# Ten hops of a graph kernel joined into one stream of groups, with the next hop's operand split on VectorE inside the stream

## What is computed

```
def step(f, _):                       # layer 0, ten times
    msg = f[src] * edge_weight[:, None]
    agg = segment_sum(msg, dst, num_segments=n)
    f = (1.0 - ALPHA) * agg + ALPHA * feat_0
    return (f, None)
out, _ = scan(step, feat, None, length=10)
...
x = layernorm(x + layer0(x))          # then layer 1 (edge MLP), layer 2, layer 3
agg = segment_sum(features[src] * ci[src][:, None], dst)   # layer 2, once
agg = segment_sum(h[src] * norm[:, None], dst)             # layer 3, once
```

## Time and profile before

| | |
|---|---|
| median of 3 runs | 9384.44 us (9378.69 to 9385.2) |
| profiled execution | 9374.58 us, span 9372.8 us |
| PE busy | 7891.7 us (84% of the span) |
| DVE busy | 6697.0 us (71%) |
| POOL busy | 5318.3 us (57%) |
| ACT busy | 4324.7 us (46%) |
| ten hops, first rounding copy to last add | 1774.1 to 5971.3 us |

### The profile page before, as it was taken

The page is one execution under the profiler, slowest core; times in us unless marked ns, Lnnn a source line. Parts: engine busy times, 40 slices in busy tenths (PEclk is TensorE's granted clock), DMA queues, the critical chain, the costliest instruction groups (busy, mean ns, idle before and its releaser), DMA issues. The chain is left out here.

```text
span 9372.8 us, 552081 instructions
## 1 busy us (share of the span) xinstructions
PE 7891.7 (84%) x229013; PEld 6623.7 (71%) x229013; DVE 6697.0 (71%) x13250; ACT 4324.7 (46%) x9003; POOL 5318.3 (57%) x5427
## 2 busy tenths in 40 slices
PE   4957667798989989898988989599999999598595
PEld 4956657798988889898988889444444444387494
DVE  6788888887877878787877878644444444586487
ACT  1249879644444444444444444244444444343142
POOL 2410000276766767676766767477777777375074
PEclk6569955699999999999999999799999999798597
DMA  5300055698988989898988989633332233196195
GB/s 83 97 22 0 6 182 228 252 312 284 312 287 291 304 282 312 285 313 286 311 285 292 300 284 312 184 77 79 79 79 77 77 80 79 41 306 215 60 317 165
DMA packets 572216, 1835.96 MB, mean 196 GB/s; under 512 B 215006, under 2 KB 276470, under 8 KB 570238
## 3 DMA queue, kind: packets, MB, share of 16 engines
q1 hardware_dynamic: 492926, 1779.79, 57.0%
q0 software_dynamic: 59776, 46.03, 3.4%
q10 hardware_dynamic: 19328, 7.36, 0.5%
HBM read 1667.65 MB, written 160.19 MB: 195 GB/s over the span
## 5 line engine op out<-in xcount | busy, mean ns | idle before, releaser
L1282 POOL TENSOR_TENSOR arena<-arena 128x768 f32<-128x768 f32 (+2 forms) x1800 | 2739.5, 1522 | 2821.8 <-DVE arena L1338 2804.7
L1251 ACT CAST arena<-banks 128x384 bf16<-128x384 f32 (+1 forms) x3600 | 1991.8, 608 | 2734.5 <-DVE banks L1334 2734.5
L1370 PE MATMUL banks<-arena 128*128 128x48 bf16 x58800 | 2510.2, 184 | 10.4 <-issue 10.4
L1370 PEld LDWEIGHTS banks<-arena 128*128 128x128 fp8e4 x58800 | 2352.1, 96 | 59.4 <-issue 58.0
L1382 PE MATMUL banks<-arena 32*128 32x144 bf16 x118800 | 2288.5, 224 | 59.7 <-issue 42.8
L1338 DVE TENSOR_TENSOR arena<-banks,arena 128x384 f32<-128x384 f32 (+1 forms) x3600 | 1930.4, 567 | 557.7 <-ACT arena L1251 557.1
L1370 PE MATMUL banks<-xc,arena 128*128 128x48 bf16 x24500 | 2069.2, 185 | 271.8 <-issue 118.1
L1370 PEld LDWEIGHTS banks<-xc,arena 128*128 128x128 fp8e4 x24500 | 1911.5, 96 | 408.2 <-issue 162.0
L1334 DVE TENSOR_TENSOR banks<-banks,wslot 128x384 f32<-128x384 f32 (+1 forms) x3600 | 1880.2, 568 | 222.3 <-PE banks L1370 212.3
L1382 PEld LDWEIGHTS banks<-arena 32*128 32x128 bf16 x118800 | 1937.5, 92 | 142.8 <-issue 50.4
L1638 POOL DMA_INDIRECT f<-node_table,idx x1568 | 1559.8, 995 | 556.3 <-issue 462.6
(11 more groups left out here) (359 smaller groups left out, 9986.3 us busy)
## 6 DMA issues: line engine op xcount, KB each, us to landing
arena<-onehots SPq DMA_DIRECT2D x1200, 768.0 KB, 4.7
arena<-onehots SPq DMA_DIRECT2D x300, 864.0 KB, 4.8
arena<-onehots SPq DMA_DIRECT2D x300, 800.0 KB, 4.3
arena<-in_dst SPq DMA_DIRECT2D x195, 512.0 KB
onehots<-arena SPq DMA_DIRECT2D x100, 768.0 KB, 3.2
arena<-key_rows SPq DMA_DIRECT2D x196, 196.0 KB
node_table<-xc SPq DMA_DIRECT2D x11, 2352.0 KB, 17.7
f<-node_table,idx POOLq DMA_INDIRECT x1568
```

The source lines that it names most:

```text
L1251: m = nc.scalar.copy(as_bank(mp_b[:, b % 3, 0, tiles, :, 1]), bank)
L1282: nc.gpsimd.tensor_tensor(mp[:, b % 3, 2, 0:NTILE[b], :], mp[:, b % 3, 1, 0:NTILE[b], :], mp_b[:, b % 3, 1, 0:NTILE[b], :, 1], ALU.subtrac ...
L1370: m = nc.tensor.matmul(to, hot[:, i * P:(i + 1) * P], x_part, start=c == 0, stop=c == 2)
```

## The change

`spmm` takes the number of hops and runs them as one stream of 250 groups; PE has a single loop over them and no longer knows of hops. What a hop's end did is spread over the groups:

- At the end of each group but the first of a hop, DVE splits the four blocks that POOL finished last (`split_next`: two subtractions of 192 columns, SBUF to SBUF, in the spare buffer `next_rest`). The last hop leaves this out.
- In the last group of a hop DVE and ACT each copy five batches' worth of the next operand over the old one, one after each gather (`move`); the sixth batch (`LATE`), which holds the last destinations, follows in the next hop's first group, ahead of b3.
- POOL's three additions stand after the low part of b2 (one) and of b3 (two); in a hop's first group all three stand after that of b1. The overflow gather of a hop's first group waits for two stores of the table (82 and 16 blocks), which SP issues between its fetches.
- The three parts of a weighted row lie packed: 48 high parts side by side, then the 48 float32 rests, whose halves are middle and low. ACT therefore writes 48 neighbouring bf16 numbers instead of every second one, PE's scatter reads 144 neighbouring bf16 numbers, and POOL's low part is written in place as bf16. `SUM_PARTS` picks the parts out of the sums by a step of two.

```
-            with nc.Fori(0, HOPS):
-                spmm(xc_raw, f01_raw, True)
+            spmm(xc_raw, f01_raw, HOPS)
...
+                    def split_next(g, d):
+                        cols = bass.ds(d * (QB4 * D), QB4 * D)
+                        dve.wait_ge(added_up, g * 3 + 6)
+                        nc.vector.tensor_tensor(next_rest[:, cols], accD_raw[:, cols], acc_top[:, cols], ALU.subtract).then_inc(next_resting, 1)
+                        dve.wait_ge(next_resting, g + 1)
+                        nc.vector.tensor_tensor(next_low[:, cols], next_rest[:, cols], next_top[:, cols], ALU.subtract).then_inc(next_split, 1)
+
+                    def move(h, b, groups):
+                        dve.wait_ge(next_split, h * NGRP + groups)
+                        nc.vector.tensor_copy(x_rest[:, batch(b)], next_rest[:, batch(b)]).then_inc(rest_moved, 1)
...
+                            if enters and b == 3:
+                                split_next(g - 1, NGRP - 1)
+                                move(h - 1, LATE, NGRP)
+                            dve.wait_ge(g_done, n + 1)
+                            if leaves and b != LATE:
+                                move(h, b, EARLY_GROUPS)
...
+                        if h + 1 < hops and (not isinstance(d, int) or d > 0):
+                            split_next(g - 1, d - 1)
...
-                                nc.gpsimd.tensor_tensor(mp[:, b % 3, 2, 0:NTILE[b], :], mp[:, b % 3, 1, 0:NTILE[b], :],
-                                                        mp_b[:, b % 3, 1, 0:NTILE[b], :, 1], ALU.subtract).then_inc(lo_done, 1)
+                            nc.gpsimd.tensor_tensor(mp_low[:, b % 3, 0:NTILE[b], :], mp_rest[:, b % 3, 0:NTILE[b], :],
+                                                    mp_mid[:, b % 3, 0:NTILE[b], :], ALU.subtract).then_inc(lo_done, 1)
...
-                                m = nc.scalar.copy(as_bank(mp_b[:, b % 3, 0, tiles, :, 1]), bank)
+                                nc.scalar.copy(mp_high[:, b % 3, tiles, :], bank).then_inc(top_done, 1)
...
-                                m = nc.tensor.matmul(banks[:, 4 + q, 0:3 * D], hot[rows, i * P:(i + 1) * P], mp_b[rows, b % 3, :, i, :, 1],
+                                m = nc.tensor.matmul(banks[:, 4 + q, 0:3 * D], hot[rows, i * P:(i + 1) * P], mp_b[rows, b % 3, i, :],
...
-                            if i == 0 or s % XBL == 0:
-                                pe.wait_ge(x_ready, s // XBL + 1)
```

More of the change, by code:

```diff
@@ new lines, in _ @@
+                    for h in range(hops):
+                        for b in range(NBATCH):
+                            fetch(h * NGRP, 0, b)
+                            if h and b == 1:
+                                store(h, 0, FIRST_TILE[LATE], EARLY_GROUPS)
+                        for b in range(NBATCH):
+                            fetch(h * NGRP + 1, 1, b)
+                            if h and b == 0:
+                                store(h, FIRST_TILE[LATE], NB, NGRP)
+                        with sp.Fori(2, NGRP) as d:
+                            for b in range(NBATCH):
+                                fetch(d + h * NGRP, d, b)
@@ L1229, in _, with copy_sums @@
                 @block.scalar
                 def _(act):
-                    if again:
-                        for c in range(XCH):
-                            nc.scalar.copy(x_raw[:, chunk(c)], accD_raw[:, chunk(c)]).then_inc(x_taken, 1)
-                    def copy_sums(d):
-                        act.wait_ge(s_done, d * NBATCH + 3)
-                        act.wait_ge(added_up, d * 3)
+                    def copy_sums(g):
+                        act.wait_ge(s_done, g * NBATCH + 3)
+                        act.wait_ge(added_up, g * 3)
@@ L1237, in copy_sums @@
                         act.sem_inc(top_seen, 1)
                         nc.scalar.copy(group_sums[:, :].rearrange("p (q f) -> p q f", q=QB4), banks[:, 4:8, 0:3 * D]).then_inc(evac, 1)
-                    def turn(d, first):
+                    def move(h, b, groups):
+                        act.wait_ge(added_up, 3 * (h * NGRP + groups + 1))
+                        act.sem_inc(move_seen, 1)
+                        nc.scalar.copy(x_raw[:, batch(b)], accD_raw[:, batch(b)]).then_inc(x_moved, 1)
@@ L1298, in _ @@
[L1298 to L1300 removed]
+                    nc.gpsimd.tensor_copy(idx_now[:, 0:1], idx_ov[:, 0:1]).then_inc(ov_picked, 1)
+                    for h in range(hops):
+                        turn(h * NGRP, 0, h)
+                        with pool.Fori(1, NGRP) as d:
+                            turn(d + h * NGRP, d, h)
                 @block.vector
                 def _(dve):
[L1304 to L1309 removed]
@@ L1345, in _, with split_x @@
[L1345 to L1348 removed]
+                    def split_x(b):
+                        nc.vector.tensor_tensor(x_rest[:, batch(b)], x_raw[:, batch(b)], x_top[:, batch(b)], ALU.subtract).then_inc(x_resting, 1)
+                        dve.wait_ge(x_resting, b + 1)
+                        nc.vector.tensor_tensor(rest_low[:, batch(b)], x_rest[:, batch(b)], rest_top[:, batch(b)], ALU.subtract).then_inc(x_ready, 1)
@@ new lines, in _ @@
+                    for b in range(X_AHEAD):
+                        split_x(b)
+                    dve.sem_inc(r_done, 4)
+                    for h in range(hops):
+                        turn(h * NGRP, 0, h, False, h > 0)
+                        with dve.Fori(1, NGRP - 1) as d:
+                            turn(d + h * NGRP, d, h, False, False)
+                        turn(h * NGRP + NGRP - 1, NGRP - 1, h, h + 1 < hops, False)
+                    dve.wait_ge(s_done, hops * NGRP * NBATCH + 3)
```

285 lines of the change are left out of this document (144 added, 141 removed).

## The result

The changed kernel takes **9280.09 us** (median of 4 runs, 9278.54 to 9283.24) against 9383.85 for the kernel before beside it (4 runs): a ratio of 0.9891, 95% interval 0.988 to 0.9903. The profiled execution has 9278.54 us against 9374.58, so 96 us less, where 40 were forecast; the median had been forecast at 9344. The gain is more than twice the forecast one, and the miss is 56 us by the profiled executions.

A forecast was written before the change was run, and what follows sets the result against it. PE was taken to bound groups inside a hop (15.18 of 15.64 us), with joints costing 28.9 us each. Saving 198 and losing 158 gave 9334, plus 9.9 for the median: 9344 us; own case 9290 to 9400, whole range 9180 to 9475.

The forecast's parts named there:

- The pair and POOL's instruction: At a group's end DVE's second subtraction waits for POOL's b5 low part at the shared port: 1.87 us a group.
- Rival 1: POOL late enough or DVE's pair slips in first: groups stay at 15.64, 198 us won, 9186; chance 0.12.
- A group with a split ahead takes 16.4 us: Mid-hop groups, delayed by DVE's pair, take 16.4 instead of 15.64 us: 198 x 0.8 = 158 us lost.
- the second of the two that the prediction followed: Delay reaching PE through POOL's low part of b0: 1.87 + 0.2 - 1.07 - 0.22 = 0.78 us a group.
- rival 3: POOL's low part slower in rows of 48, 0.4 us at the upper bound: 1.38 us a group, 9459; chance 0.20.
- The prediction's first way: Delay through b0, b1 and ACT's copy of the sums, needed before PE's scatter of b0: 0.78 us a group.
- Layers 2 and 3 and the tenth hop stay at PE's 15.64: Groups without a split ahead, bound by PE, keep their 15.64 us; no gain or loss counted.
- a shorter scatter as a sign of being wrong: The prediction called itself wrong if PE's scatter gets shorter in the changed profile.
- rival 2: Packed operand speeds up PE's scatter, 74 to 66 ns for four matmuls: 0.8 us a group, 9204; chance 0.10.
- The joints: Between two hops, 7.3 us a joint instead of 28.9: 21.6 x 9 = 194 us saved.
- the wait for the overflow rows: In a hop's first group, DVE waits at b5 for rows behind the second store: 1 to 1.5 us more.
- Rival 4: Joints stay dear, stores land late or new code comes late to DVE: 10 us more each, 9434; chance 0.12.

The follow-up runs named there:

- layout_only_2: The kernel before with the packed layout alone, without the stream, the split or the moved additions: 9321.61 us, ratio 0.9927 to the kernel before.

## Why the prediction was right in its direction and 56 us too cautious

The starts of b5's overflow rows on DVE (L1325 before, L1377 after) cut both traces into the same pieces:

| stage (us) | before | after | change in all | forecast |
|---|---|---|---|---|
| up to the first hop's b5 | 1803.9 | 1797.3 | -7 | -4 |
| 198 groups with a split ahead, mean | 15.62 | 16.09 | +93 | +158 |
| nine joints, three groups each, mean | 76.3 | 57.5 | -168 | -194 |
| tenth hop, layers 2 and 3, 69 groups | 1073.4 | 1053.7 | -20 | 0 |
| layer 1, which the change leaves alone | 2264.0 | 2270.6 | +7 | 0 |

**The pair and POOL's instruction: right.** The second subtraction lasts 1.46 us beside POOL and 0.38 without, in two places; the pair costs 1.89 us where 1.87 was worked out from the earlier trace rows. The Trainium skill, "SBUF — State Buffer", section "SBUF: two separate sides", has the two engines share the ports as a lock held for a whole instruction. The trace agrees: the end of L1356 lies 0.23 us behind that of POOL's L1316 in the shown group, and sharing in halves would have given twice 0.38 and not 1.46. Rival 1, no hindrance, falls.

**The step that failed: "A group with a split ahead takes 16.4 us", 198 x 0.8 = 158 us lost.** The way was right, the size was not: a group took 16.07, 0.43 above 15.64 and not 0.78, and the 198 lost 93 us. (The 15.62 of the table is a little under 15.64 because 19 groups of the kernel before were shorter, as told above.) The way that binds is the second of the two that the prediction followed, by POOL's low part of b0, and along it every term can be measured:

| term, us | forecast | measured |
|---|---|---|
| the pair | +1.87 | +1.89 |
| POOL's low parts slower in rows of 48, two of them | +0.20 | 0 |
| DVE's b5 and b0 shorter | -0.22 | -0.34 |
| slack ahead of the scatter of b0 that is used up | -1.07 | -1.00 |
| PE's three scatters from b0 on | 0 | -0.12 |
| together | +0.78 | +0.43 |

POOL's low part takes 1.47 us as before, so rival 3, the slower low part, falls. DVE gains 0.26 us by ACT's shorter casts and 0.08 because the weighting of b0 may start 0.08 us before the printed end of b5's rests. The slack was 2018.96 - 2017.83 = 1.13 us; of it the 0.13 of the handover stay. The prediction's first way, by ACT's copy of the sums, does not bind: the copy ends at 2313.46, before POOL's low part.

**The second failed step, inside the first and beside it: "Layers 2 and 3 and the tenth hop stay at PE's 15.64", and under it that PE's work does not change.** The operand with a step of two made every scatter 0.04 us longer, and the prediction had itself named a shorter scatter as a sign of being wrong. This was rival 2, at a third of its size: 0.8 us a group had been put there, 0.23 to 0.29 came (15.64 to 15.41 in layout_only_2, mostly 15.64 to 15.36 in the tenth hop, 15.38 to 15.09 in layers 2 and 3, which never stood at 15.64). That is the 20 us of the table, and the 0.12 us of the held groups are another 24.

Two readings had stood against rival 2. One was the row: 72 matmuls in 1.34 us were taken as 74 ns for four, but the time from the first start to the last end holds the length of one matmul, 0.22 us, besides. The packed rows show it: 64, 68 and 72 matmuls take 1.18, 1.24 and 1.30, so four more cost about 60 ns. In the traces the fours of a scatter start 65 ns apart before and 62 to 63 ns apart in layout_only_2, where 144 columns at 2.4 GHz are 60. So 5 ns a four could be won, not 14, and the step was half of them. The other was the Trainium skill ("TensorE: Matmul & The Clock Gate", section "Measured speedup vs the span model": 4 ns of issue for each further row tile). As an estimate by that rule four matmuls of 144 columns span 72 ns. The tiles of a four do start 3 to 5 ns apart in layout_only_2, which agrees; but the next four starts well before 72 ns are over, so the rule, which is for one pack, does not say what a long row of packs takes, and it could not speak against rival 2.

**The joints: mis-sized the other way.** From the hop period, 411.2 - 22 x 16.07 = 57.7 us for the three groups at a joint, 10.8 above three of 15.64, where 7.3 were kept; the table has 57.5, and 26 us less gain than forecast. The term that was off is the wait for the overflow rows, 4.05 us in the first joint and 37.1 in all nine, where 1 to 1.5 had been put: the second store needed 5.7 us to land behind SP's fetches, not 4, and 4.3 us a joint is what it costs to have the stores at all. Rival 4, dear joints, is true in this part, at a third of its 10 us.

By the table the held groups gave 65 us more than forecast, the free ones 20 and the first start 3, the joints 26 less, and layer 1 took 7 more in this execution: 55 of the 56 us. It is in part luck that the miss is not larger: the joints' shortfall covers some of the groups' excess.

**Not settled.** The idle at PE's turn was 0.46 in the old code and stayed at 0.45 when the operand was packed, so that there all of the gain came through (64 us). In the new code it went from 0.48 to 0.31 when the step was put back, and 18 to 22 us were left. Why it trades against the matmuls' length in one code and not in the other, and why one text has both 0.25 and 0.48, no run here tells. That a turn of 700 matmuls is not fetched anew and one of 1,400 is, is shown; that the idle has to do with it is not.

## What to carry to other kernels

A VectorE subtraction of two SBUF operands that meets a GpSimd one here ends only after it (1.46 against 0.38 us, beside one of 1.60): put it where GpSimd is idle, such as the wait between two roundings, before asking whether the time saved is worth its place. When you compare many equal matmuls with what their columns give, take the time between their starts, and not the whole time divided by their number; if that is a few per cent above, look at the operand's step. And before unrolling a TensorE loop, see how much code a turn has: doubling it here made the kernel a third slower.

## What the runs showed of the hardware

- A PE loop of some 700 matmuls a turn fetched 0.74 MB of instructions on q8 in the whole program; of some 1,400 a turn, 31.80 MB, and PE stood still up to 8.8 us at a time: 9091 to 12139 us.
- PE's moving operand with a step of two bf16: 64 row-tiled matmuls of 144 columns in 1.20 to 1.22 us, against 1.18 without a step. One run of 144 or three of 48 make no difference without a step (1.18 both); with it they differ by 0.01.
- ACT's cast of 384 PSUM columns takes 481 ns into neighbouring bf16, against 596 into every second. The row by form of the changed kernel, count, busy us and mean ns:

```profile
L1269 ACT CAST arena<-banks 128x384 bf16<-128x384 f32 x2700 | 1284.5, 481 | 2141.3 <-DVE banks L1382 2138.5 <-PE banks L1430 2.8
```

- A DVE subtraction that waits for the one before it starts 0.18 us after it ends inside the loop, where its addresses come from registers; at the joint, with fixed addresses, 2199.65 + 0.36 to 2200.05, 0.04 us. No run changes the addresses alone.
- POOL's subtraction of 768 columns takes 1.47 us in one run with float32 output and in rows of 48 with bf16 output.
